# One core, four attention and feed-forward layers: a new order of steps for each engine, inside the stages too

## The reference

```python
x = x + jnp.tanh(g_xattn[0]) * _L0_xattn_ref(_layernorm(x, axis=-1), ctx_1024, ...)
x = x + jnp.tanh(g_ffn[0]) * _L0_ffn_ref(_layernorm(x, axis=-1), ...)
x = x + jnp.tanh(g_xattn[1]) * _L1_xattn_ref(_layernorm(x, axis=-1), ctx_1024, ...)
...
x = x + jnp.tanh(g_ffn[3]) * _L3_ffn_ref(_layernorm(x, axis=-1), ...)
return x
```

## Time and profile before

| what | value |
|---|---|
| median of three runs | 931.37 us (930.12 to 935.81) |
| the profiled execution | 930.08 us, its span 928.3 us |
| busy in the span: PE, DVE, ACT, POOL | 840.6 (91%), 761.9 (82%), 555.3 (60%), 309.7 (33%) us |
| mean granted clock of PE | 0.957 of full |
| matmuls and weight loads | 5288 each |
| DMA | 14.12 MB, 5.1% of the 16 engines' span on the main queue |

### The profile page before, as it was taken

How to read it: one execution, slowest core, us unless ns; L and a number is a source line. 1 busy time by engine, 2 the same in 40 slices (tenths; PEclk the granted TensorE clock), 3 DMA queues, 4 the chain that set the end, 5 groups by cost and what they waited for, 6 DMA issues and landing times.

```text
span 928.3 us, 16914 instructions
## 1 busy us (share of the span) xinstructions
PE 840.6 (91%) x5288; PEld 651.0 (70%) x5288; DVE 761.9 (82%) x1907; ACT 555.3 (60%) x1077; POOL 309.7 (33%) x507
## 2 busy tenths in 40 slices
PE   4999887899999999999999999999979989978796
PEld 2677665666666665688878788778767779867574
DVE  4799789979999999699899899788887755465886
ACT  2577565567777776676656565577755534423474
POOL 2544216313444433231222122433421253321143
PEclk9899899879999999899999999999998999998998
DMA  4100010000000000110000000020001000000001
GB/s 139 24 1 2 1 28 1 25 1 26 26 25 26 22 23 2 23 27 2 0 1 1 1 1 1 0 75 2 1 2 43 2 1 1 1 1 1 1 12 34
DMA packets 26005, 14.12 MB, mean 15 GB/s; under 512 B 11047, under 2 KB 25406, under 8 KB 25918
## 3 DMA queue, kind: packets, MB, share of 16 engines
q1 hardware_dynamic: 25918, 13.04, 5.1%
HBM read 11.99 MB, written 1.05 MB: 14 GB/s over the span
## 4 chain that ended last, share of the span: by engine, by line
PE 47%; DVE 8%; issue 3%; ACT 3%; POOL 0%; DVEq 0%; ACTq 0%; POOLq 0%
PE bank L1842 4%; PE bank L1844 3%; PE bank L1843 3%; PE bank L796 2%; PE bank L1317 2%; PE bank L1898 2%; PE bank L1899 2%; PE bank L1897 2%; PE bank L1272 2%; PE bank L1282 2%; PE bank L1295 2%; PE bank L1253 1%; PE bank L729 1%; PE bank L707 1%; PE bank L756 1%
## 5 line engine op out<-in xcount | busy, mean ns | idle before, releaser
L891 ACT ACTIVATE L_pt<-bank 128x512 f32<-128x512 f32 x224 | 127.2, 597 | 40.2 <-PE bank L765 27.4
L513 POOL TENSOR_TENSOR L_kc<-L_kc_all,const 128x256 fp32r<-128x256 f32 x96 | 59.4, 623 | 134.2 <-PE bank L765 76.7
L878 ACT ACTIVATE L_part<-bank,L_bias_ca,const 128x256 fp32r<-128x256 f32 x128 | 68.8, 563 | 38.4 <-PE bank L685 37.0
L1799 POOL TENSOR_TENSOR L1f_xg_lo<-L1f_xg_raw,L1f_xg_hi 128x512 fp32r<-128x512 f32 x32 | 42.0, 1312 | 146.7 <-ACT L1f_xg_hi L1947 141.9
L1024 DVE TENSOR_REDUCE L_ms<-bank 128x2 f32<-128x512 f32 x128 | 84.0, 685 | 6.3 <-PE bank L714 6.0
L1941 ACT ACTIVATE L1f_a<-bank 128x512 f32<-128x512 f32 x88 | 52.4, 599 | 46.9 <-PE bank L1844 46.4
L2063 DVE TENSOR_TENSOR L1f_h_lo<-L1f_h,L1f_h_hi 128x512 fp32r<-128x512 f32 x88 | 75.2, 859 | 6.2 <-ACT L1f_h_hi L1952 5.8
L1022 DVE TENSOR_REDUCE L_mc<-bank 128x8 f32<-128x512 f32 (+1 forms) x96 | 65.1, 679 | 10.0 <-PE bank L707 5.5
L1952 ACT CAST L1f_h_hi<-L1f_h 128x512 fp32r<-128x512 f32 x88 | 54.3, 618 | 17.9 <-DVE L1f_h L2058 17.9
L714 PE MATMUL bank<-L_k,L_q 32*128 32x256 f32 x256 | 55.0, 332 | 5.1 <-DVE L_ms L1024 4.8
L1010 DVE SCALAR_TENSOR_TENSOR L_q<-bank,L_bias_c,L_part 128x256 fp32r<-128x256 f32 x96 | 47.3, 493 | 14.5 <-ACT L_part L878 12.7
(11 more groups left out here) (427 smaller groups left out, 2603.3 us busy)
## 6 DMA issues: line engine op xcount, KB each, us to landing
L_raw<-in_L_ffn_w_dram SPq DMA_DIRECT2D x8, 176.0 KB, 2.3
L_raw<-in_L_ffn_v_dram SPq DMA_DIRECT2D x8, 176.0 KB, 2.5
L_raw<-in_L_ffn_w_dram SPq DMA_DIRECT2D x6, 192.0 KB, 3.1
x<-in_x_dram SPq DMA_DIRECT2D x4, 256.0 KB, 4.5
mask<-in_mask_Bx1xSxS_ff_dram SPq DMA_DIRECT2D x2, 512.0 KB, 4.7
out_dram<-x SPq DMA_DIRECT2D x4, 256.0 KB, 2.3
const<-in_const_dram SPq DMA_DIRECT2D x1, 964.0 KB, 5.7
ctx_rows<-in_ctx_dram SPq DMA_DIRECT2D x1, 256.0 KB, 3.0
```

The lines of the kernel that those rows point to most:

```text
L513: pool.tensor_tensor(kc[:, g], kc_all[:, g, bass.ds(b, 1)].bitcast(F32).to_broadcast([P, GH, S2]), pr.c("head4").unsqueeze(2).to_broadcast ...
L878: last = act.activation(part[:, i].bitcast(F32R), b_proj[:, i * S:(i + 1) * S], ACT.Identity, bias=bias_ca[:, i, g:g + 1], scale=pr.c("ak" ...
L891: act.activation(pt[:, g // 2, (g % 2) * NS + (HEADS_1[i] if own_keys else i)], b_st[(g * NS + i) % 2][:], ACT.Exp, scale=scale).then_inc( ...
```

## The change

Only `PLACES` is another: it now holds 1553 moved steps (PE 676, DVE 417, ACT 375, POOL 85), which lie all through the program. Every engine has the same steps as before, each once, and SP's list with all DMAs is the same. What a step does and what it waits for is unchanged. Of the table, three lines before and after:

```diff
-        (('att0', 'turn', 0), *of("att0", ('p_kc', 2))),
-        (('att0', 'p_kc', 3), *of("att0", ('proj', 0, 1))),
+        (('att0', 'p_kc', 1), *of("att0", ('p_kc', 2))),
+        (('att0', 'p_kc', 3), *of("att0", ('turn', 1))),
...
+        (('att0', 'weights', 1, 1, 0), *of("att0", ('scores', 2, 0, 0))),
```

More of the change, by code:

```diff
@@ L2713 @@
[L2713 to L2719, removed]
@@ L2757 @@
[L2757 to L2760, removed]
-        (('att1', 'scores', 1, 1, 4), *of("att1", ('pv', 0, 0, 4))),
-        (('att1', 'scores', 7, 3, 0), *of("att1", ('weights', 7, 1, 1))),
-        (('att1', 'scores', 7, 3, 3), *of("att1", ('scores', 7, 3, 4))),
@@ new lines @@
+        (('att3', 'weights', 0, 1), *of("ffn2", ('y_turn', 3))),
+        (('att3', 'context_values', 1), *of("att3", ('proj', 1, 0), ('sums', 0))),
+        (('att3', 'scores', 1, 1), *of("att3", ('turn', 2))),
+        (('att3', 'pv', 0, 1), *of("att3", ('maxima', 1))),
+        (('att3', 'divide', 0, 1), *of("att3", ('proj', 2, 0))),
+        (('att3', 'maxima', 2), *of("att3", ('pv', 1, 0), ('turn', 3))),
+        (('att3', 'divide', 1, 0), *of("att3", ('divide', 1, 1))),
+        (('att3', 'pv', 1, 1), *of("att3", ('proj', 3, 0), ('context_values', 3))),
@@ new lines @@
+        (('att3', 'weights', 2, 1), *of("att3", ('y', 1), ('sums', 2))),
+        (('att3', 'pv', 2, 0), *of("att3", ('turn', 4))),
+        (('att3', 'divide', 2, 1), *of("att3", ('maxima', 3), ('context_values', 4), ('proj', 4, 0))),
+        (('att3', 'proj', 4, 1), *of("att3", ('y', 2), ('sums', 3), ('turn', 5))),
+        (('att3', 'scores', 4, 1), *of("att3", ('context_values', 5), ('proj', 5, 0))),
+        (('att3', 'divide', 3, 0), *of("att3", ('divide', 3, 1))),
+        (('att3', 'weights', 4, 1), *of("att3", ('y', 3), ('sums', 4))),
@@ new lines @@
+        (('att2', 'maxima', 7, 1), *of("att2", ('y', 5))),
+        (('att2', 'scores', 7, 3, 0), *of("att2", ('maxima', 7, 2))),
+        (('att2', 'o_norm', 6), *of("att2", ('maxima', 7, 3))),
+        (('ffn2', 'weights', 1), *of("ffn2", ('scale', 1), ('turn', 0))),
+        (('ffn2', 'weights', 2), *of("att2", ('y', 6)), *of("ffn2", ('moments', 2))),
+        (('ffn2', 'turn', 1), *of("att2", ('o_norm', 7))),
+        (('ffn2', 'split', 0), *of("ffn2", ('scale', 3))),
+        (('ffn2', 'mul', 2), *of("ffn2", ('mul', 3), ('turn', 2))),
@@ new lines @@
+        (('att3', 'divide', 1, 0), *of("att3", ('divide', 1, 1))),
+        (('att3', 'scale', 4), *of("att3", ('y', 1)), *of("ffn3", ('moments', 0))),
+        (('att3', 'sums', 2), *of("att3", ('parts', 2))),
+        (('att3', 'scores', 3, 1), *of("att3", ('turn', 4), ('divide', 2, 0))),
+        (('att3', 'maxima', 3), *of("att3", ('divide', 2, 1))),
+        (('att3', 'scale', 5), *of("att3", ('y', 2))),
+        (('att3', 'sums', 3), *of("att3", ('turn', 5))),
+        (('att3', 'parts', 3), *of("att3", ('scale', 6))),
@@ new lines @@
+        (('att1', 'weights', 7, 0, 4), *of("att1", ('values', 7), ('maxima', 7, 2))),
+        (('att1', 'weights', 7, 1, 2), *of("att1", ('pv', 6, 1, 4))),
+        (('att1', 'weights', 7, 2, 1), *of("ffn1", ('turn', 0))),
+        (('att1', 'weights', 7, 3, 1), *of("ffn1", ('route', 0, 0))),
+        (('att1', 'weights', 7, 3, 2), *of("att1", ('pv', 7, 0, 4))),
+        (('att1', 'weights', 7, 3, 4), *of("att1", ('on_turn', 6), ('pv', 7, 1, 4))),
+        (('ffn1', 'g', 1), *of("ffn1", ('gated', 0))),
@@ new lines @@
+        (('ffn0', 'split', 5), *of("att1", ('keys', 0, 0))),
+        (('ffn0', 'split', 11), *of("att1", ('p_rstd', 0), ('keys', 0, 1))),
+        (('ffn0', 'split', 13), *of("att1", ('turn', 0))),
+        (('att1', 'keys', 1, 0), *of("att1", ('p_rstd', 1))),
+        (('att1', 'keys', 3, 2), *of("att1", ('turn', 1), ('turn', 2), ('turn', 3))),
+        (('att1', 'p_rstd', 2), *of("att1", ('spread', 3))),
+        (('att1', 'keys', 4, 0), *of("att1", ('keys', 4, 1))),
+        (('att1', 'keys', 5, 2), *of("att1", ('p_rstd', 3))),
```

1267 lines of the change are left out of this document (915 added, 352 removed).

## The result

The changed kernel took **973.51 us** (median of four runs: 942.04, 953.06, 993.96, 995.68) beside 933.59 for the kernel before on the same chip. A second set of four gave 977.22 (941.87 to 998.46). It is slower; I had said 915 and at most 931. The profiled execution is the one of 953.06, its span 951.3.

The account below looks back on a forecast made before the run. Waits of the busier of PE and DVE, both near nine tenths busy in the attentions, were taken as the room: 28.0 us of waits go, less 4 for switches and 8 given back, 16 us; 915 us, range 899 to 931.

Parts of the forecast that it names:

- The failed step: Whole kernel: no data moved or work removed, so only waits go, at most the idle time read from the profile.
- the array switches decide: Rival, second attention: 93 more array-shape switches at 0.22 us each add 20.5 us, giving 941 us; chance 0.10.
- My charge of 4 us for switches: Second attention: 93 added array-shape switches cost PE 8.4 to 20.5 us; half of the lower end charged, 4 us.
- Last seam: Into the last feed-forward: preparation moved earlier removes PE's 7.85 us wait; 7.5 for it plus 1.0 for clock, 8.5 us.
- Second batch of the fourth attention: At 751.95: PE's 2.57 us wait behind a slow DVE copy beside POOL operations; 1.0 us gained, ends 0 and 2.6.
- Last route: At 864.26: PE's 3.20 us wait behind DVE's routing, now spread further; 1.5 us gained, ends 0 and 3.2.
- Start: Zeroing on POOL goes first, bo later, cutting PE's 2.27 us wait for the first key tile; 2.0 us gained.
- first attention and seam: Idle time inside the first attention, 4.0 us of 7.0, and in the seam 100 to 140, 1.5 of 5.3.
- Routes: Second feed-forward: more down and g products give PE work during DVE's routing; 3.0 us gained, ends 0 and 4.6.
- third attention: Inside the third attention: splitting pairs of products and weights recovers 2.0 us of 5.0 idle.
- Insides: Inside the second attention: splitting pairs so DVE's next scores come sooner recovers 4.5 us of 12.9 idle.
- Given back: Whole kernel: in-order engines hand on small delays, so three tenths of the 28 us do not come; 8 us.

Follow-up runs that it names:

- experiment 7: Changed kernel, own-key scores on all 128 rows: 902.41 us, with before's second-attention order 901.39; own-key weights on all rows too: 883.45, with before's order 887.36.
- experiment 3: Changed kernel with its own order, own-key scores reading all 128 rows instead of 32: 902.41 us, ratio 0.9675.
- experiment 8: Changed kernel, only TensorE's second-attention list altered to bunch full-array products: little bunched 943.59 us, much bunched 982.89, unaltered beside them 977.22.
- the fill: Changed kernel with before's second-attention order, plus four more full-array products in each group of its batches 0 and 1: 902.38 us, ratio 0.969.

## Why the prediction was wrong

**What the low clock costs.** Two runs of the changed kernel have spans of 940.3 and 992.2 us at mean clocks of 0.919 and 0.861. At two levels, 1.00 and 0.50, that is 2 x (1 - 0.919) x 940.3 = 152 us at half clock and 276: 51.9 us longer for 124 us more, 0.42 us for each. What follows is an estimate from this price. With the low clock taken out, before stands at 894.8 (928.3 - 0.42 x 79.8), the changed kernel at 875.4 (951.3 - 0.42 x 180.7) and the version with the old second attention at 874.7. The order itself thus gained some 19 us, where I had forecast 16; the clock took 42 more than before in the profiled execution (0.42 x 100.9), and up to 82 in others (0.42 x 196). The price is not the same everywhere: a line through the 63 runs of the kernel before gives 0.37 and 899 us without low clock, and the gain is then 24. That this lies near the 16 is in part luck, since the terms below came out one by one larger and smaller than forecast.

- *The failed step* is the claim that "the sum of work stays; only waits can go", with the whole clock read from before as if the order could not change it. I had the earlier trace rows before me with a clock of 0.94 in the second attention, and wrote only that a lower mean clock "would cost on top". So the clock of the second attention stood at nothing in the sum, without a reason, and it was the largest term: 42 us in the profiled execution. In the second attention PE was busy 266.11 of 270 us at 0.72, with the same products as before at 0.94.
- *The rival "the array switches decide"* had the sign and the place (the second attention, waits for L714, which went from 6.0 to 39.3 us), and the wrong mechanism. At full clock the pace is 8.2 to 8.4 products in a microsecond in both orders; 252 switches were slower than 323, though with waits of their own; and its price of 20.5 us was under half of the 42. My charge of 4 us for switches is of the size by which the two pairs of experiment 7 differ, 4.9 (3.9 faster against 1.0 slower), but one of these pairs ran on two chips.
- *Last seam*, 8.5: right in its wait (7.85 to none, and the stretch at 0.50 behind it is gone). With the 1.0 and 1.5 for the fourth attention and last route I had 11.0, against some 14.6 by difference.
- *Second batch of the fourth attention*, 1.0: wrong as a place. The slow DVE instruction is one beside a large POOL instruction; the delay moved from a copy (2.42 us) to the normalization (4.62) and PE waits 2.89. *Last route*, 1.5: 3.20 became 1.20.
- *Start*, 2.0, first attention and seam, 5.5: together 3.9 measured, not told from nothing. The end that I named, "the first maxima could instead wait", came: 2.18 us. *Routes*, 3.0, and third attention, 2.0: together 2.8 measured, not told from nothing, though the two waits named went.
- *Insides*, 4.5 for the second attention: 3.9, only where clock and row switches are out of the way. In the kernel as it stands, less than nothing.
- *Given back*, 8: over all but the second attention I had 23.5, less its share of 6.7 gives 16.8, and 21.3 came. The 16.8 lies within its interval of 15 to 27, so the runs do not say whether the charge was too high.

## What to carry to other kernels

Before reordering a TensorE-bound stage of small-tile products, look at the granted clock there. In this kernel it already fell now and then in the second attention, and the order decided how long it stayed down; one half-clock microsecond cost some 0.4 us, and in all that took more than every wait of the forecast could give (42 to 82 us against 28). Let a small product take the full array where the computation allows it (experiment 3, shown), and try to keep full-array products in bunches (experiment 8, not shown). Even added, thrown-away full products paid: 40 us in the changed kernel, 5 in the kernel before. A schedule fitted to durations at full clock should be judged by several runs, since the eight of the changed kernel lie between 942 and 998 us, and by stage: here the quickest versions with the right output stand at 901 to 902 us (0.9655 to 0.969 of before). They are the old second attention with full score rows, the same with the fill instead, and the new order with full score rows.

## What the hardware showed that I had not expected

- The granted clock can stand at 0.50 for 54.6 us while PE has no idle time at all (190 to 245 us: busy 54.99 of 55).
- The clock depends on the rows used: the same products in the same order with 128 instead of 32 rows took 902.4 instead of 973.5 us, and with the last 32-row products gone, 883.5.
- A full-array product and one of 32 rows have the same columns, but not the same effect: by the medians 128 more of the one made the kernel 40 us faster, of the other 3 us, within its scatter.
- Two small DVE instructions (L1384, 128x128 each) took 4.62 us while POOL ran one of 4.24, against 0.60 elsewhere. In the kernel before it was a copy that took 2.42 us beside such an instruction, against 0.18: the cost stayed with the POOL instruction and changed the one that paid it.
